# A decay column as bias of the exponential, routing tables and routed experts planned later, a scatter in two pieces

## The chip, the cores and the metric

The kernel runs on one core of a Trainium2 chip. The metric is the device time of one execution in microseconds, taken as the median of several runs.

## The reference

Two layers, each of the form x = x + attention(norm(x)) * silu(experts(norm(x))), all in float32. Layer 0 is softmax attention with eight experts. Nearly all of the change is about layer 1, on 2 x 512 tokens of width 256: linear attention by a gated delta rule, and two shared and sixteen routed experts of which each token takes two.

```python
beta  = sigmoid(x @ W_b.T)
decay = exp(-softplus(x @ W_a.T + dt_bias) * exp(A_log))     # one per token and value head
kk    = kk / norm(kk)
def step(state, inp):                    # 16 key heads, 2 value heads each, 128 x 128 states
    Sk    = k_t . state
    delta = (v_t - Sk) * b_t
    state = state * d_t + outer(k_t, delta)
    o     = q_t . state
# o is normed, multiplied by silu(z), projected by W_out
probs = softmax(xt @ W_router);  top_v, top_i = top_k(probs, 2)
routed_out = sum over the two experts of gelu(xt @ Wrt_up[e]) * gate @ Wrt_down[e]
```

## The kernel before

The scan is done in chunks of 128 tokens. A **unit** u (0 to 63) is key head h = u // 4, chunk i = u % 4, and takes both batches and both value heads at once, which makes four lanes of 128 columns. In a unit the decay between two tokens of a chunk is the exponential of a difference of running sums of logarithms: a row (the sum at one token, along the columns) plus a column (the negative sum at the other, one number for each partition). `row` fetches the rows of the four lanes from DRAM (`crow`) into RC on all partitions (L1256), `dec` adds the column `cumb` on GpSimd (L2786), puts -1e30 where the later token would come first (affine_select, L2789), and takes the exponential on ScalarE (E, L2544). `gram` multiplies keys by keys and by queries (L1612) and VectorE multiplies with E (L2232). From the result an inverse of a triangular matrix is built by doublings (L1633 to L1656, with VectorE's ZL, ZF, R, and ScalarE's XYLM), then W (L2292), and the state update (KS, U, so: L1674 to L1704, with ScalarE's D, QSc, De). Heads 0 and 1 (units 0 to 7) do all doublings unit by unit; from head 2 on the inner 16 x 16 blocks of four units are inverted together (`dg`, `iv1`, `p8`, `iv2`, `q8`, `iv3`), `xc` copies them on ScalarE (L2551), and `sx` scatters them to `parked` in DRAM by 16 DMAs of SyncE (SP; L1285), 8 blocks by 2 matrices. `ld` loads the unit's matrices back from there.

Each head needs projections of keys, queries, values and gates (L1339), three convolution taps each on VectorE (L2148), and its output projection (L1737, L1745).

The **routed experts**: `top` finds the two best experts of each token (L1807 to L1820, VectorE and one ScalarE operation), `cnt`, `own`, `tiles`, `hits`, `slot` (L1832 to L1891, VectorE, with small matmuls L1562 to L1574) make the tables that sort tokens by expert into 31 tiles. Eight groups `g` of four tiles follow: gathers of rows and weights by indirect DMAs of GpSimd (L2729, L2745), transposes (L1583), products (L1592, L1600), a gelu, and a store of the results (`ss`, L1222). At the end `cb` gathers each token's two results (L2755) and adds them up on VectorE (L2198).

**What sets the order.** All this is listed as parts with an engine, an estimated cost, what they depend on, and a rank (about the unit number beside which the part belongs). `Plan.arrange` is a list scheduler: it takes again and again the part that can begin first by its own estimates, in steps of 0.0517 us; among equals the lower rank goes first. The result is a fixed order for each engine and a fixed assignment of PSUM banks. Each engine runs its list in order and waits with semaphores. The dictionaries `RANK` and `LATER` shift the rank and the beginning of each kind of part on each engine.

```python
begin = at + self.HOLD if p.eng == "PE" and p.label[0] in self.THIN and thin > self.CAP else at
key = int((begin + p.later) * (1 / self.GRAIN)), p.rank, p.no
```

## Time and profile before

| | |
|---|---|
| runs, us | 1229.45, 1229.77, 1232.14 (median 1229.77) |
| profiled execution, us | 1230.72 |
| its span, us | 1228.9 |
| mean granted clock of TensorE | 0.982 of full |
| instructions | 28718 |
| layer 0 and the preparation of layer 1 | until about 300 us |
| units 0 to 63 | from about 300 us to the end |

The profile is of one execution; its span is the time from the first to the last recorded instruction. Engines are named PE (TensorE; PEld its weight loads), DVE (VectorE), ACT (ScalarE), POOL (GpSimd), SP (SyncE, its queue SPq). PEclk is the clock granted to TensorE as a share of full speed. "x8" is a number of instructions; in a timeline, a bracket at the end gives the engine's idle time before the instruction and what ended it. Matmuls overlap, so their single durations add up to more than their busy time.

### The profile page before, as it was taken

What the parts mean: (1) busy time and instruction counts of PE and PEld (TensorE: products, weight loads), DVE (VectorE), ACT (ScalarE), POOL (GpSimd) and SP (SyncE); (2) the same over time, 40 slices, a digit from 0 to 9 for tenths busy, and PEclk for the clock granted to TensorE, in tenths of its full rate; (3) what the DMA queues carried; (4) which work ended last, traced back from release to release, by engine and by line L of the source; (5) the groups of instructions that cost most, each with busy time, mean ns of one, the idle gap of its engine ahead of it and who ended that gap; (6) DMA issues with size and microseconds to landing.
All of it is one profiled execution on the core that took longest, in us unless ns stands there. A gap on an engine that the chain in (4) does not pass through costs nothing. (4 is left out here: it accounts for less than half of the span.)

```text
span 1228.9 us, 28718 instructions
## 1 busy us (share of the span) xinstructions
PE 1159.3 (94%) x9866; PEld 977.3 (80%) x9866; DVE 1047.5 (85%) x2365; ACT 841.6 (68%) x2396; POOL 863.4 (70%) x1101
## 2 busy tenths in 40 slices
PE   8898999888799899999999999999999999999997
PEld 7654566666698888989898988888888888888886
DVE  5796356899988989898988999899899889999988
ACT  4014643477487678877787778777877787787775
POOL 4115342839879888797969888787878787867634
PEclk9999999889799999999999999999999999999999
DMA  7942122214226556565636375655454663626331
GB/s 232 249 122 102 49 74 74 86 40 150 84 78 161 119 169 149 156 188 132 190 94 207 94 214 143 189 146 152 141 163 130 179 171 90 186 56 208 73 117 44
DMA packets 219492, 165.94 MB, mean 135 GB/s; under 512 B 103572, under 2 KB 186772, under 8 KB 219348
## 3 DMA queue, kind: packets, MB, share of 16 engines
q1 hardware_dynamic: 214612, 149.82, 44.0%
q0 software_dynamic: 4736, 14.29, 3.9%
q8 instruction: 79, 1.29, 0.4%
q14 instruction: 65, 0.53, 0.1%
HBM read 115.71 MB, written 48.16 MB: 133 GB/s over the span
## 5 line engine op out<-in xcount | busy, mean ns | idle before, releaser
L2556 ACT ACTIVATE XYLM<-ps 128x512 f16<-128x512 f32 x216 | 125.9, 598 | 54.1 <-PE ps L1647 53.1
L2148 DVE SCALAR_TENSOR_TENSOR KQ<-ps,cw,KQ 128x511 f32<-128x511 f32 (+2 forms) x192 | 140.6, 742 | 12.7 <-ACT KQ L2492 11.0
L2148 DVE SCALAR_TENSOR_TENSOR yv<-ps,cw,yv 128x511 f32<-128x511 f32 (+2 forms) x192 | 139.8, 741 | 8.6 <-ACT yv L2492 6.7
L1339 PE MATMUL ps<-XH,WVh 128*128 128x256 f32 (+1 forms) x384 | 133.5, 348 | 7.1 <-ACT KN L2507 4.5
L1339 PE MATMUL ps<-XH,WVl 128*128 128x256 f32 (+1 forms) x384 | 122.9, 320 | 0.0
L1339 PE MATMUL ps<-XL,WVh 128*128 128x256 f32 (+1 forms) x384 | 122.8, 320 | 0.0
L2590 ACT ACTIVATE sq<-O 128x128 bf16<-128x128 f32 x256 | 79.5, 310 | 28.7 <-DVE O L2328 14.5
L2596 ACT ACTIVATE O<-O,small 128x128 f32<-128x128 f32 x256 | 82.1, 400 | 14.2 <-POOL small L2834 14.0
L2278 DVE TENSOR_TENSOR ZL<-ps,cst 128x256 f16<-128x256 f32 x192 | 77.9, 415 | 10.4 <-PE ps L1633 8.9
L1339 PEld LDWEIGHTS ps<-XH,WVh 128*128 128x128 f32 x384 | 72.8, 190 | 12.8 <-ACT KN L2507 5.4
L2853 POOL TENSOR_TENSOR OGL<-O,OGH 128x512 fp32r<-128x512 f32 x62 | 80.6, 1300 | 2.8
L1704 PEld LDWEIGHTS ps<-De,PT 128*128 128x128 f32 x512 | 75.5, 193 | 5.7
L2786 POOL TENSOR_TENSOR RC<-RC,dec 128x512 f32<-128x512 f32 x64 | 67.2, 1051 | 17.0 <-DMA RC<-crow 16.8
L1704 PE MATMUL ps<-De,PT 128*128 128x128 f32 x512 | 77.8, 277 | 0.0
L1339 PEld LDWEIGHTS ps<-XH,WVl 128*128 128x128 f32 x384 | 72.5, 189 | 5.8
L1339 PEld LDWEIGHTS ps<-XL,WVh 128*128 128x128 f32 x384 | 72.9, 190 | 3.3
L2578 ACT ACTIVATE D<-ps,dec 128x128 f32<-128x128 f32 x192 | 60.9, 378 | 20.6 <-PE ps L1690 18.9
L2439 ACT ACTIVATE PT<-ps 128x1024 f32<-128x1024 f32 (+3 forms) x64 | 44.1, 705 | 43.8 <-PE ps L1436 41.8
L2834 POOL TENSOR_TENSOR small<-small 128x4 f32<-128x4 f32 (+1 forms) x66 | 67.4, 1021 | 5.5
L1737 PE MATMUL ps<-WOh,OGH 128*128 128x256 f32 x248 | 67.2, 304 | 2.9 <-DVE O L2347 2.9
L1612 PE MATMUL ps<-KQ 128*128 128x256 f32 x256 | 68.2, 389 | 0.2 <-ACT st L2604 0.2
L2565 ACT ACTIVATE QSc<-ps,dec 128x128 f32<-128x128 f32 x192 | 59.4, 377 | 13.1 <-DVE RH L2304 12.8
(359 smaller groups left out, 4083.0 us busy)
## 6 DMA issues: line engine op xcount, KB each, us to landing
XYLM<-parked SPq DMA_DIRECT2D x56, 512.0 KB, 5.3
RC<-crow SPq DMA_DIRECT2D x128, 128.0 KB, 4.7
decayed<-PTE SPq DMA_DIRECT2D x64, 256.0 KB, 3.4
PT<-decayed SPq DMA_DIRECT2D x64, 256.0 KB, 3.1
parked<-LM SPq DMA_DIRECT2D x56, 256.0 KB, 4.9
WV<-in_WV SPq DMA_DIRECT2D x16, 512.0 KB, 4.1
exr<-in_ex SPq DMA_DIRECT2D x16, 384.0 KB, 3.9
WK<-in_WK SPq DMA_DIRECT2D x16, 256.0 KB, 3.0
```

The lines of the kernel that those rows point to most:

```text
L1339: m = pe.matmul(o, a, b, start=c + k == 0, stop=c == 1 and k == 2)
L1612: m = pe.matmul(ps[:, bk, 256 * b:256 * b + 256].rearrange("p (k t) -> p k t", k=2), K[:, h % 3, at], KQ[:, h % 3, :, at], start=True, sto ...
L1704: m = pe.matmul(ps[:, bk, 256 + 128 * v:384 + 128 * v], PT[:, u % 2, 2 * b + v, :], De[:, b, v, :], start=True, stop=True)
L1737: pe.matmul(ps[:, bk, 256 * b:256 * b + 256], OGH[:, 2 * b + v, :], weights[:, h % 2, v, :], start=v + k == 0, stop=False, skip_group_chec ...
L2148: m = dve.scalar_tensor_tensor(out=dst[:, k:512], in0=ps[:, bk, 0:512 - k], scalar=cw[:, h, j, 3 - k:4 - k], in1=dst[:, k:512], op0=ALU.mu ...
L2278: leave(dve.tensor_tensor(half(zl(k), k, 0), p, lv(k), ALU.mult), "a", u, k)
L2556: leave(act.activation(changed(u, k), ps[:, bank("b", u, k), :].rearrange("p (c n t) -> p c n t", c=2, t=1 << (k - 1)), ACT.Copy), "b", u, k)
L2590: act.activation(sq[:, 1, :], O[:, u % 2, l, :], ACT.Square, accum_out=so[:, u % 2, l:l + 1]).then_inc(s_sqo, 1)
L2596: m = act.activation(O[:, u % 2, l, :], O[:, u % 2, l, :], ACT.Copy, scale=ro[:, u % 2, l:l + 1])
L2786: pool.tensor_tensor(rc.rearrange("p (b v) t -> p b v t", b=2), rc.rearrange("p (b v) t -> p b v t", b=2), bias.unsqueeze(3).broadcast_to( ...
L2834: pool.tensor_tensor(ro[:, u % 2, four], ro[:, u % 2, four], mh[:, four], ALU.pow).then_inc(s_ro, 1)
L2853: pool.tensor_tensor(OGL[:], O[:, u % 2], OGH[:].bitcast(F32), ALU.subtract).then_inc(s_ogl, 1)
```

## The change

1. `dec`: GpSimd's addition of the column is gone, and the select alone remains. ScalarE takes the exponential lane by lane, four instructions of 128x128 with the column as bias, where one of 128x512 stood; it now waits itself for the column (`s_dd`).
2. `top` moves from rank -4 to 4 and 5, the tables from rank 2 to 7, 7.5, 8, 8.5 and 8.6, the groups of routed experts from 1 + 5.5g to 9 + 5g, and the final combining from 45 to 48.
3. `sx` becomes `sx` and `sy`, each of eight DMAs (first matrix 0 of all blocks, then matrix 1), two parts in SP's list; `xc` and `ld` wait for both.
4. The estimated costs of `dec` and `sx` in the plan follow (POOL 1.83 to 0.7, ACT 0.53 to 1.08; SP 7.9 to twice 3.95), and nearly every entry of `RANK` and `LATER` has another value.

```diff
 RANK = {
-    "KS": {"ACT": 15.02}, "KS:first": {"ACT": 149.13, "DVE": 1181.68, "PE": 1010.25},
+    "KS": {"ACT": 22.36}, "KS:first": {"ACT": -215.27, "DVE": 22.74, "PE": -258.01},
...
-HEADS = ("ck", "ck1", "ck2", "ck3", "cq", "cq1", "cq2", "cq3", "cv", "cv1", "cv2", "cv3", "kn", "kb", "kns", "Vt", "Zt", "dg", "iv1", "p8", "iv2", "q8", "iv3", "xc", "sx")
+HEADS = ("ck", "ck1", "ck2", "ck3", "cq", "cq1", "cq2", "cq3", "cv", "cv1", "cv2", "cv3", "kn", "kb", "kns", "Vt", "Zt", "dg", "iv1", "p8", "iv2", "q8", "iv3", "xc", "sx", "sy")
...
-                                              rank + RANK.get(phase(label), {}).get(eng, 0.0), int(takes) if n == 0 else 0)
+                                              round(rank, 6) + RANK.get(phase(label), {}).get(eng, 0.0), int(takes) if n == 0 else 0)
...
-    P.add(("top", 1), -4, ("DVE", 1.5, (("rt1",), "DVE")), ("ACT", 1.6))
-    P.add(("top", 2), -4, ("DVE", 4.5, (("top", 1), "ACT")))
+    P.add(("top", 1), 4, ("DVE", 1.5, (("rt1",), "DVE")), ("ACT", 1.6))
+    P.add(("top", 2), 5, ("DVE", 4.5, (("top", 1), "ACT")))
...
-    P.add(("dec", u), rank, ("POOL", 1.83, (("row", u), "DMA"), (("pre", 4), "DVE")),
-          ("ACT", 0.53, earlier(1, "pt", "DVE"), (("cc", 1), "POOL")))
+    P.add(("dec", u), rank, ("POOL", 0.7, (("row", u), "DMA")),
+          ("ACT", 1.08, earlier(1, "pt", "DVE"), (("cc", 1), "POOL"), (("pre", 4), "DVE")))
...
-    P.add(("sx", h), rank + 0.2, ("SP", 7.9, (("xc", h), "ACT")), ("DMA", 0.3))
+    P.add(("sx", h), rank + 0.2, ("SP", 3.95, (("xc", h), "ACT")), ("DMA", 0.3))
+    P.add(("sy", h), rank + 0.2, ("SP", 3.95, (("xc", h), "ACT")), ("DMA", 0.3))
...
-    P.add(("own",), 2, ("DVE", 3.0, (("cnt",), "DVE")))
-    P.add(("tiles",), 2, ("DVE", 3.4, (("own",), "DVE")))
-    P.add(("hits",), 2, ("DVE", 2.4, (("tiles",), "DVE")))
+    P.add(("own",), 7.5, ("DVE", 3.0, (("cnt",), "DVE")))
+    P.add(("tiles",), 8, ("DVE", 3.4, (("own",), "DVE")))
+    P.add(("hits",), 8.5, ("DVE", 2.4, (("tiles",), "DVE")))
...
     for g in range(GROUPS):
-        rank = 1 + 5.5 * g
+        rank = 9 + 5 * g
...
-    rank = 1 + 5.5 * GROUPS
+    rank = 8 + 5 * GROUPS
...
-                        for k in range(2):
-                            sp.dma_start(parked[h % 2, k, at, :, at].rearrange("r q c -> q r c"),
-                                         XY16[at, k, :].rearrange("q (r c) -> q r c", c=16)).then_inc(d_sx, 16)
+                        sp.dma_start(parked[h % 2, 0, at, :, at].rearrange("r q c -> q r c"),
+                                     XY16[at, 0, :].rearrange("q (r c) -> q r c", c=16)).then_inc(d_sx, 16)
+                elif what == "sy":
+                    w.wait_ge(d_l1, 128)
+                    w.wait_ge(s_xc, 2 * (h - LEAD + 1))
+                    for b in range(8):
+                        at = slice(16 * b, 16 * b + 16)
+                        sp.dma_start(parked[h % 2, 1, at, :, at].rearrange("r q c -> q r c"),
+                                     XY16[at, 1, :].rearrange("q (r c) -> q r c", c=16)).then_inc(d_sx, 16)
                 elif what == "ld":
                     w.wait_ge(d_sx, 256 * ((h - OWN) // 4 + 1))
...
-                    act.activation(E[:, :, 1:129], RC[:, u % RCS], ACT.Exp).then_inc(s_E, 1)
+                    w.wait_ge(s_dd, 9)
+                    for l in range(4):
+                        c = 128 * (l // 2) + 32 * (u % 4) + 2 * (u // 4) + l % 2
+                        m = act.activation(E[:, l, 1:129], RC[:, u % RCS, l, :], ACT.Exp, bias=cumb[:, c:c + 1])
+                    m.then_inc(s_E, 1)
...
                     w.wait_ge(d_row[u % RCS], 32 * (u // RCS + 1))
-                    w.wait_ge(s_dd, 9)
-                    pool.tensor_tensor(rc.rearrange("p (b v) t -> p b v t", b=2), rc.rearrange("p (b v) t -> p b v t", b=2),
-                                       bias.unsqueeze(3).broadcast_to((128, 2, 2, 128)), ALU.add).then_inc(s_rel, 1)
-                    w.wait_ge(s_rel, nth("POOL", *x))
                     pool.affine_select(out=rc, in_=rc, compare_op=ALU.is_ge, fill=-1e30, base=0,
                                        pattern=[[0, 4], [1, 128]], channel_multiplier=-1).then_inc(s_lag, 1)
```

## Rows read from the trace of the kernel before

**Rows 1.** Page, part 1: busy time, share of the span and instructions of each engine.

```profile
PE 1159.3 (94%) x9866; PEld 977.3 (80%) x9866; DVE 1047.5 (85%) x2365; ACT 841.6 (68%) x2396; POOL 863.4 (70%) x1101
```

**Rows 2.** Windows of 50 us: length, busy time (instructions) by engine, PEclk, DMA share, GB/s.

```profile
300.00:350.00 50.00, 38.18 (x433) 33.19 (x432) 45.41 (x101) 28.08 (x82) 42.79 (x49) 0.83 0.32 89
350.00:400.00 50.00, 47.96 (x479) 42.70 (x477) 42.55 (x90) 38.29 (x108) 42.87 (x58) 1.00 0.47 124
400.00:450.00 50.00, 45.81 (x410) 41.90 (x407) 45.76 (x101) 35.55 (x109) 40.36 (x50) 0.97 0.57 149
450.00:500.00 50.00, 46.00 (x416) 40.70 (x415) 43.34 (x97) 37.13 (x109) 44.05 (x56) 1.00 0.63 172
```

**Rows 3.** Windows of other lengths, same columns.

```profile
302.70:323.30 20.60, 10.83 (x86) 9.16 (x87) 18.88 (x32) 5.32 (x18) 17.70 (x18) 0.64 0.25 77
...
323.00:350.00 27.00, 25.15 (x295) 22.19 (x293) 24.14 (x62) 20.63 (x61) 22.79 (x29) 0.96 0.36 96
600.00:1100.00 500.00, 492.04 (x4385) 437.58 (x4385) 451.87 (x1024) 389.55 (x1189) 407.19 (x517) 1.00 0.54 149
```

**Rows 4.** Timeline of VectorE: start, duration in us, operation, idle time before it.

```profile
244.66 0.28 DVE L1807 TENSOR_REDUCE small<-s 128x8 f32<-128x128 f32 x1
...
248.50 1.74 DVE L2117 RECIPROCAL dec<-dec 128x256 f32<-128x256 f32 x1
...
301.84 0.28 DVE L1832 SCALAR_TENSOR_TENSOR st<-ps,cst 128x128 f32<-128x128 f32 x1
...
309.52 0.68 DVE L2292 SCALAR_TENSOR_TENSOR W<-ps,XYLM 128x512 f32<-128x512 f32 x1
...
314.84 3.96 DVE L1891 SCALAR_TENSOR_TENSOR st<-cst,small 128x2048 f16<-128x2048 f32 x1
```

**Rows 5.** Timeline of TensorE, same columns.

```profile
251.46 0.79 PE L1339 MATMUL ps<-XH,WVh 128*128 128x512 f32 x1 [4.54 <-ACT KN L2507]
...
310.34 2.04 PE L1690 MATMUL ps<-V,W 128*128 128x128 f32 x8 [4.58 <-DVE W L2292]
...
319.20 0.40 PE L1644 MATMUL ps<-ZL,XYLM 128*128 128x64 f16 x4 [2.34 <-DVE ZL L2278]
...
364.67 1.06 PE L1690 MATMUL ps<-V,W 128*128 128x128 f32 x8
```

**Rows 6.** Tile RC (ns min/median/max, starts; waits), then ScalarE's timeline.

```profile
L2786 POOL TENSOR_TENSOR RC<-RC,dec x64: 1033/1044/1324, 265.6 to 1126.8; 128x512 f32<-128x512 f32 x64
L2789 POOL TENSOR_SCALAR_AFFINE_SELECT RC<-RC x64: 636/642/907, 266.8 to 1128.0; 128x512 f32<-128x512 f32 x64
...
  POOL RC L2789: 4.4, 6
...
281.68 0.63 ACT L2544 ACTIVATE E<-RC 128x512 f32<-128x512 f32 x1
...
324.97 1.28 ACT L2596 ACTIVATE O<-O,small 128x128 f32<-128x128 f32 x4 [0.93 <-POOL small L2834]
```

**Rows 7.** VectorE's L2148 by source line (ns min/median/max); GpSimd's timeline.

```profile
L2148 DVE SCALAR_TENSOR_TENSOR KQ<-ps,cw,KQ x192: 716/742/752, 208.5 to 1097.2; 128x511 f32<-128x511 f32 x64, 128x510 f32<-128x510 f32 x64, 128x509 f32<-128x509 f32 x64
...
316.79 2.51 POOL L2812 TENSOR_SCALAR_AFFINE_SELECT XYLM<-XYLM 128x512 f16<-128x512 f16 x1
```

**Rows 8.** Timeline of SyncE's queue: issues.

```profile
457.30 7.85 SPq L1285 DMA_DIRECT2D parked<-XY  x16
465.26 0.37 SPq L1299 DMA_DIRECT2D PT<-decayed  x1
```

**Rows 9.** Windows of L1592 alone and of L1600 alone; tile wt by line.

```profile
350.00:400.00 50.00, 2.03 (x16) 1.86 (x16) 1.00 0.47 124
...
350.00:400.00 50.00, 2.06 (x8) 1.37 (x8) 1.00 0.47 124
...
L2755 POOL DMA_INDIRECT wt<-rows_out,posi x12: 955/1033/1119, 972.6 to 1174.5; - x12
L2198 DVE SCALAR_TENSOR_TENSOR KQ<-wt,small,KQ x12: 472/482/1504, 1136.2 to 1198.2; 128x256 f32<-128x256 f32 x12
```

More of the change, by code:

```diff
@@ L134 @@
[L134 to L136 removed]
[4 rows of a table removed]
[L141 removed]
+    "KS": {"ACT": 22.36}, "KS:first": {"ACT": -215.27, "DVE": 22.74, "PE": -258.01},
+    "KS:last": {"ACT": 280.22, "DVE": 252.3, "PE": 210.41}, "U": {"ACT": 50.18},
@@ new lines @@
+    "gram:first": {"DVE": -67.68, "PE": -12.72}, "gram:last": {"DVE": -517.09, "PE": -1250.23},
+    "gt": {"ACT": 520.96, "PE": -897}, "hits": {"DVE": -53.08}, "iv1": {"DVE": -1477.56}, "iv2": {"DVE": -6.87},
+    "iv3": {"DVE": -326.24}, "kb:first": {"POOL": -503.43}, "kn": {"ACT": 206.3, "POOL": 107.57},
+    "kn:first": {"ACT": -0.06, "PE": -26.86, "POOL": 808.85}, "kns": {"ACT": 112.77},
+    "ld": {"DMA": 211.49, "SP": -612.6}, "ld:last": {"DMA": 55.72, "SP": -10.09},
+    "ln1": {"ACT": 378.5, "DVE": 269.03, "PE": -405.47}, "ls": {"DMA": -79.98},
@@ L142 @@
+    "yl:last": {"DVE": -291.41, "PE": 170.61},
 }
 LATER = {
[L146 to L150 removed]
@@ new lines @@
+    "own": {"DVE": 0.04}, "pd": {"SP": 0.18}, "pd:last": {"SP": 0.08}, "pf": {"DVE": 0.63, "SP": 2.39},
+    "pl:last": {"POOL": 0.03}, "pm:last": {"POOL": 1.31}, "ps:first": {"DMA": 1.52, "SP": 1}, "ps:last": {"SP": 0.05},
+    "py": {"POOL": 0.23}, "r:first": {"PE": 0.04}, "r:last": {"DVE": 0.13}, "rb:0": {"SP": 0.69},
+    "rc:1": {"DVE": 1.5}, "rd:0": {"SP": 0.02}, "rd:1": {"SP": 0.37}, "row:first": {"DMA": 1.39, "SP": 1.22},
+    "row:last": {"SP": 0.13}, "sc:1": {"ACT": 0.21, "PE": 0.01}, "slot": {"DVE": 0.17}, "small": {"SP": 2.48},
@@ L536, in plan_inverse @@
     if u >= OWN:
-        P.add(("ld", u), rank - 0.5, ("SP", 0.45, (("sx", h), "DMA"), earlier(3, "c", "DVE")), ("DMA", 2.2))
+        P.add(("ld", u), rank - 0.5, ("SP", 0.45, (("sx", h), "DMA"), (("sy", h), "DMA"), earlier(3, "c", "DVE")), ("DMA", 2.2))
     P.add(("pd", u), rank + 0.5, ("SP", 0.45, (("ps", u), "DMA"), earlier(2, "so", "PE", 0), earlier(2, "so", "PE", 1)), ("DMA", 0.8))
```

142 lines of the change are left out of this document (61 added, 81 removed), and 23 rows, old and new, of the table RANK.

## The prediction

> **What bounds the kernel now.** I read the page first. TensorE is busy in 94% of the span, VectorE in 85%, GpSimd in 70%, ScalarE in 68% [rows 1]. The mean hides where time is lost, so the table by stage comes next. From 600 to 1100 us TensorE is busy in 492.04 of 500 us, at a clock of 1.00 [rows 3]. There it sets the pace, VectorE being second with 90%, and GpSimd (81%) and ScalarE (78%) have room. Before that TensorE has holes: it is busy 38.18 of 50 us at 300 to 350, with a granted clock of 0.83, and misses 2.04 us of 350 to 400, 4.19 of 400 to 450 and 4.00 of 450 to 500 [rows 2]. So a change is worth something if it closes early holes, and next to nothing if it only takes load from GpSimd after 500 us.
>
> The finer windows, among which also that long one stands, put the hole at 302.7 to 323.3 us. There TensorE is busy 10.83 of 20.60 us at a mean clock of 0.64, while VectorE is busy 18.88 [rows 3]. The timeline says with what: the routing tables (L1832 to L1891) start at 301.84 and end at 318.80. Between them stand only three operations of the main work, R (0.68), W (0.68) and one ZL (0.42) [rows 4] (of the three, W is shown). TensorE's rows name them as what it waited for: W 4.58 us, ZL 2.34 us. And the matmuls that it does run go at its lower level (1.2 of 2.4 GHz): eight matmuls of L1690 take 2.04 us here and 1.06 us at 364.67 [rows 5].
>
> **The change part by part. Tables.** They are 318.80 - 301.84 = 16.96 us of VectorE less 1.78 for the three operations, 15.2 us, moved from rank 2 to ranks 7 to 8.6, that is beside units 7 to 9 instead of unit 1. The hole: 10.83 us of busy TensorE at mostly half rate is about 6.2 us at the full rate (10.83 x 1.06/2.04 = 5.6, a little more since part ran fast). In the next window, 323 to 350, TensorE is busy 25.15 of 27 us [rows 3], 93%; at that share the 6.2 us of work want 6.7, at worst twice that, because this work is a chain of dependent steps. The gain is 20.6 - 6.7 = 13.9 at best, 20.6 - 13.4 = 7.2 at worst; I take 11 us. It is passed on to the end, since TensorE afterwards is the pacemaker and what it did not do there it must do later.
>
> The same 15.2 us come back at the new place. Between 400 and 500 us VectorE has 4.24 + 6.66 = 10.9 us free and TensorE misses 8.2 us already [rows 2]. If all free time of VectorE served the tables, TensorE would pay 15.2 - 10.9 = 4.3 us; if none did, 15.2 us, if its queued matmuls of projections bridge all of it, 0. The longest piece is hits, 3.96 us, the others are parts of 2.4 to 3.4 us in the plan, so the main work gets in between them, which it got only three times before. I take 5.
>
> **Top two.** L1807 to L1820 (244.66 to 248.50, 3.84 us) stand before the reciprocal L2117 of the decay chain, which starts at 248.50, the moment they end [rows 4]. Moved to ranks 4 and 5, they let this chain start up to 3.8 us earlier. But TensorE's own stall there, 4.54 us, waits for ScalarE's KN [rows 5], and while the decays are computed it has projections to do. Gain between 0 and 3.8; I take 1, nearer to the row of KN.
>
> **Decay.** GpSimd loses L2786, 64 x 1.044 us = 67 us, and keeps the select L2789 (0.642). ScalarE has four 128x128 activations instead of one 128x512. The trace has no exponential with a bias column. The one now takes 0.63 us; nearest to the four is L2596, 128x128 with a column as scale, four in 1.28 us [rows 6]. That adds 0.65 us a unit, 64 x 0.65 = 42 us in all. The bounds: the four handle the elements of the one, so they add no less than 0, and if each took as long as the one, 1.9 us, 121 us in all; the row of L2596 has the very shape, so I take its 42. ScalarE has 110 of 500 us free [rows 3], some 215 over the 978 us after 250; 42 fit in, but the engine drains PSUM banks, and an eviction behind the four comes up to 0.65 us later. On the other side E comes 1.04 - 0.65 = 0.4 us sooner after its row has landed, the wait for the column moves from GpSimd's queue to ScalarE's (where drains of projections stand behind it, once, near 262 us), and ScalarE waited for the select only 6 times, 4.4 us in all [rows 6]. The row of unit u + 2 is fetched into the buffer that E of unit u frees, so a later E also makes that fetch later; the two offset each other within the unit. The gain is at most 4.4, the loss, if a twentieth of the added 42 us shows in TensorE's waits, 2, and if a fifth of twice that shows, 17. I take 0 net.
>
> Here a rule can be weighed. The main VectorE operation L2148 keeps within 716 and 752 ns over 192 runs, whatever GpSimd does, while GpSimd's select took 2.51 us beside hits, against 0.64 elsewhere [rows 6, 7]. So less work on GpSimd makes the taps no faster; I book 0. The Trainium skill, page "SBUF — State Buffer", section "Who interferes with whom", says that a VectorE instruction with two SBUF inputs and a GpSimd instruction that reads SBUF exclude one another for their whole length, and that one with a single SBUF input does not wait. The trace agrees with both halves. By it the tables, which read SBUF twice, would collide with GpSimd at the new place too.
>
> **Scatter in two pieces.** sx is one block of 16 issues on SP, 7.85 us at 457.30, and PT<-decayed is issued right behind it, at 465.26 [rows 8]. In two blocks (same 16 issues, same data) what is ready gets in after about 4 us, up to 3.9 us earlier. This happens 14 times, but load ld still waits for both, and may come later by whatever is put between. Bounds: the 3.9 us gained at two of the fourteen, where TensorE happens to wait for what stands behind (8), or 2 lost. I take a gain of 1.
>
> **Routed experts.** Eight groups move from ranks 1 + 5.5g to 9 + 5g, with their gathers on GpSimd's queue, four rows and four weights each, and their stores on SP's. The first group's matmuls lie between 350 and 400 us: 16 of L1592 in 2.03 us, 8 of L1600 in 2.06 [rows 9], and eight transposes, 1 us by the rate of the first. That is 5 us. Taken out of 350 to 440 us, where TensorE has holes, they go to where it is full. If nothing fills in, that costs 5 us, if projections of the next heads do, 0; I take 2. At the end, the last group moves from rank 39.5 to 44 and the combining gathers from 45 to 48, 3 units later; 64 units in the 929 us after 300 make 14.5 each, so 44 us. They begin at 972.6 now and are used from 1136.2 on [rows 9]: hidden, with 120 us of room.
>
> **Sum.** -11 + 5 - 1 + 0 - 1 + 2 = -6 us. The order of everything else is drawn anew too (nearly all of RANK and LATER); TensorE's idle time from 500 to 1200, about 10 us, bounds what that can gain, and it can lose as much; 0 to -3 is where I put it, since GpSimd, whose late work heads pieces of the chain, is freer: -2. The profiled execution took 1230.7 us (span 1228.9 and 1.8 around it; 1 more than the median of 1229.77). Against its own time the sum gives 1230.7 - 8 = 1222.7, against the median 1229.8 - 8 = 1222 us, which I forecast.
>
> **Rivals.** (A) Likeliest, the above: hole at 303 to 323 closed, part of it back at 400 to 500. (B) The stall only moves: at ranks 7 to 8.6 VectorE is 87 to 92% full, the tables cost 11 there, gain and price cancel, 1229 us. For it: VectorE's row of 400 to 450, 45.76. Against: at 302 us only the first units' chains are there to be fed, and each main result that VectorE delays stops them; at 400 us projections of later heads are queued too, and TensorE is busy 92% although VectorE is as full. (C) Slower: ScalarE becomes late. The four activations take not 1.28 but some 1.7 us, between the row and its bound, which makes 64 x 1.07 = 68 us, and they stand before drains of TensorE's banks. Once more than 8 us of it show in TensorE's waits the gain is gone; a fifth of it makes 13.6 - 8 = +5, 1235 us. For it: PSUM drains on ScalarE are what TensorE's bank waits hang on. Against: 110 of 500 us free. (D) The tables and GpSimd exclude one another at the new place, by the select's 2.51 us: three such blocks and the inner blocks of head 2 behind them delay its inverse by 3 x 1.9 = 6 us, 1228 us. The rule of the page above is this rival's. (E) Everything fits: hole closed to the best 14, the tables are free at the new place, the chain of the decays gains 3, the holes at 400 to 500 shrink by 2 more: 1211 us.
>
> **How the numbers follow.** A 0.50 (1222, its own range 1216 to 1227), E 0.17 (1211), B 0.12 (1229), C 0.15 (1235), D 0.06 (1228). The measurement tells 0.2%, 2.5 us, from no change. Faster: 0.47 of A, all of E (0.17), 0.05 of B and D, whose times have a spread too: 0.69. Same: the other 0.03 of A and 0.10 of B: 0.13. Slower: C, and 0.03 of D: 0.18. The range that leaves out 0.2 goes from 1208 to 1234.
>
> **What would show it.** TensorE busy over 45 of 50 us at 300 to 350 with a clock above 0.95; the tables' lines in pieces between 380 and 460, and TensorE missing up to 5 us more there; L2786's line gone, L2544's 64 activations become 256 of 128x128, near 0.4 us each, and ScalarE's busy time goes up by 40 to 65 us (durations overlap); the first group of experts after 430. The prediction is wrong if TensorE's total idle time does not fall, or if waits for ScalarE's drains grow by more than 10 us.

## The result: slower by 3.2%

| | before | after |
|---|---|---|
| runs, us | 1229.45 to 1237.46, median 1230.95 (4) | 1269.53 to 1272.81, median 1271.57 (4) |
| ratio to before, 95% interval | | 1.0321 [1.0292, 1.0349] |
| profiled execution and its span, us | 1230.72, 1228.9 | 1272.52, 1270.8 |
| granted clock, mean | 0.982 | 0.970 |

The forecast was 1222 us with a range to 1234. The kernel takes 1271.6, some 40 us more than before. Lines of the kernel after lie a few further on: L1704 is now L1709, L2148 is L2153, L2789 is L2792, L1891 is L1896, L2544 is L2552, L1592 is L1597.

The page, part 1 (compare [rows 1]), and the costliest group that the edit made:

```profile
PE 1171.5 (92%) x9866; PEld 985.8 (78%) x9866; DVE 1050.0 (83%) x2365; ACT 877.4 (69%) x2587; POOL 797.6 (63%) x1037
...
L2552 ACT ACTIVATE E<-RC,dec 128x128 f32<-128x128 f32 x256 | 81.9, 399 | 10.3 <-DVE PTE L2237 9.4 <-issue 0.5
```

GpSimd lost 65.8 us and ScalarE got 35.8, as the edit says. TensorE has the same 9866 matmuls, 12.2 us more busy time and 29.7 us more idle time (69.6 to 99.3).

Windows of the kernel after (compare [rows 2] and the third of [rows 3]; columns as there):

```profile
300.00:350.00 50.00, 42.96 (x485) 35.98 (x486) 47.35 (x112) 37.70 (x116) 37.95 (x52) 0.97 0.36 112
350.00:400.00 50.00, 44.57 (x487) 36.45 (x486) 43.25 (x89) 35.79 (x100) 36.97 (x49) 1.00 0.35 91
400.00:450.00 50.00, 44.97 (x357) 39.63 (x355) 38.20 (x96) 36.49 (x118) 39.20 (x46) 0.97 0.65 185
450.00:500.00 50.00, 45.85 (x420) 41.10 (x420) 39.31 (x93) 34.49 (x113) 34.58 (x45) 0.93 0.31 82
...
600.00:1100.00 500.00, 485.18 (x4284) 434.50 (x4284) 449.36 (x999) 408.21 (x1267) 381.20 (x488) 1.00 0.55 154
```

The hole at 300 to 350 did get smaller, 42.96 for 38.18, and the clock there is 0.97 for 0.83. The same holds where the tables themselves stand now (compare the first of [rows 3]):

```profile
333.10:353.70 20.60, 16.09 (x163) 13.95 (x163) 20.18 (x47) 13.28 (x44) 14.94 (x16) 0.92 0.25 72
```

Behind it things got worse, the steady stretch too: 485.18 for 492.04.

To see where the 41.9 us of span were lost, cut both traces at the same work: layer 0 until its last update of x, the preparation until the first state product of unit 0 (L1704), 286.7 us of units, the other units, the tail. Before, then after:

```profile
0.00:217.40 217.40, 201.43 (x1322) 129.76 (x1323) 142.16 (x311) 80.88 (x135) 72.93 (x93) 0.99 0.45 127
217.40:313.30 95.90, 76.06 (x517) 60.38 (x516) 84.98 (x200) 63.89 (x142) 69.37 (x101) 0.87 0.32 93
313.30:600.00 286.70, 270.05 (x2527) 241.80 (x2525) 254.30 (x572) 213.73 (x639) 242.20 (x301) 0.98 0.53 144
600.00:1217.40 617.40, 605.76 (x5476) 540.56 (x5475) 558.17 (x1267) 480.12 (x1470) 472.20 (x596) 1.00 0.51 141
```

```profile
0.00:233.70 233.70, 211.64 (x1344) 138.55 (x1344) 142.82 (x314) 83.99 (x142) 73.06 (x93) 0.93 0.43 119
233.70:326.00 92.30, 72.73 (x512) 56.65 (x513) 81.18 (x186) 63.28 (x155) 60.89 (x95) 0.91 0.30 94
326.00:612.70 286.70, 260.22 (x2399) 228.00 (x2398) 239.29 (x550) 210.12 (x656) 198.05 (x255) 0.97 0.43 123
612.70:1259.50 646.80, 620.94 (x5583) 557.60 (x5582) 579.40 (x1299) 516.82 (x1627) 459.09 (x584) 1.00 0.51 144
```

Layer 0 takes 16.3 us longer, and no line of its code was edited. The preparation gives back 3.6. The units take 933.5 us for 904.1, 29.4 more: in their first 286.7 us TensorE is idle 26.5 for 16.65 and gets 128 matmuls less done, in the others 25.9 for 11.6. So two thirds of the loss lie in the loop, spread over it, and a third in layer 0 and the preparation, whose code the change doesn't touch; it draws their order anew too.

In layer 0 the clock is 0.93 for 0.99, and 10.2 of the 16.3 us are longer busy time, a part of it because 22 more matmuls fall into the window (1344 for 1322). Windows of 10 us of the kernel after show the places; before, the same windows have 0.83, 1.00 and 1.00:

```profile
50.00:60.00 10.00, 6.16 (x33) 4.09 (x28) 4.61 (x8) 0.60 (x1) 5.58 (x6) 0.64 1.06 237
...
120.00:130.00 10.00, 7.08 (x60) 3.14 (x58) 2.93 (x6) 3.11 (x7) 4.58 (x6) 0.73 0.11 33
130.00:140.00 10.00, 9.33 (x56) 4.08 (x52) 3.48 (x5) 8.27 (x13) 3.54 (x5) 0.59 0.15 42
```

The waits say what the loop lost (engine, line, releaser: us in total, times, longest). Before:

```profile
POOL RC L2786 <- DMA RC<-crow: 16.8, 13, 3.7
...
POOL OGH L2847 <- DVE O L2347: 6.2, 4, 3.6
...
POOL LM L2806 <- DMA parked<-LM: 3.3, 2, 1.9
```

After:

```profile
POOL OGH L2850 <- DVE O L2352: 69.5, 26, 9.8
POOL RC L2792 <- DMA RC<-crow: 51.1, 21, 5.6
...
POOL LM L2809 <- DMA parked<-LM: 17.0, 7, 6.1
...
PE ps L1742 <- POOL OGH L2850: 10.8, 6, 5.4
```

GpSimd stands 26 times, up to 9.8 us, before the cast of O into OGH, because its list has the cast before O is there; what is queued behind it comes late. (Before, it stood at this cast 28.5 us in all, 22.3 of them until L1745 had let go of OGH.) TensorE's output projection L1742 waits for OGH 10.8 us in turn (before, its L1737 never did). Added up by what ended them, TensorE's waits for GpSimd grow from 4.9 to 22.9 us, those for VectorE from 36.5 to 40.2, for ScalarE from 20.8 to 24.0 and for DMAs from 1.3 to 3.1: GpSimd's share is 18.0 of the 29.7 us of added idle time. Once, at 1109 us, LM waits for a store, the second half of O stands behind it, and TensorE behind that (GpSimd's timeline, then TensorE's):

```profile
1109.34 0.61 POOL L2809 CAST LM<-M 128x512 f16<-128x512 f32 x1 [6.07 <-DMA parked<-LM]
1109.91 1.26 POOL L2856 TENSOR_TENSOR OGL<-O,OGH 128x512 fp32r<-128x512 f32 x1
...
1111.23 1.22 PE L1750 MATMUL ps<-WOh,OGL 128*128 128x256 f32 x4 [3.80 <-POOL OGL L2856]
```

And the tables? VectorE's timeline (compare [rows 4]):

```profile
263.58 1.74 DVE L2122 RECIPROCAL dec<-dec 128x256 f32<-128x256 f32 x1
...
333.10 0.28 DVE L1837 SCALAR_TENSOR_TENSOR st<-ps,cst 128x128 f32<-128x128 f32 x1
...
348.77 0.68 DVE L2352 TENSOR_TENSOR O<-ps,Z 128x512 f32<-128x512 f32 x1
349.37 0.68 DVE L2368 TENSOR_TENSOR xt<-ps,xt 128x512 f32<-128x512 f32 x1
349.96 2.31 DVE L1896 SCALAR_TENSOR_TENSOR st<-cst,small 128x2048 f16<-128x2048 f32 x1
```

They stand at 333 to 352 us, not between 380 and 460, so beside units 0 and 1, not 7 to 9. Of the shift by 31 to 35 us against [rows 4], 12.7 are the later start of the units. Top two still stands right before the reciprocal of the decay chain, which starts 15.1 us later than before.

### The profile page after: what moved, and what is told of

Same layout as the page of the kernel before. It is cut to its first block, busy times and chain, and to the rows that moved or that the text cites. A ratio compares the mean times of both kernels' runs of the same rounds, so it can differ in the third digit from the quotient of the medians.

```text
span 1270.8 us, 28912 instructions
## 1 busy us (share of the span) xinstructions
PE 1171.5 (92%) x9866; PEld 985.8 (78%) x9866; DVE 1050.0 (83%) x2365; ACT 877.4 (69%) x2587; POOL 797.6 (63%) x1037
## 4 chain that ended last, share of the span: by engine, by line
PE 42%; DVE 21%; DMA 10%; ACT 9%; POOL 7%; issue 7%; SPq 4%; DVEq 0%; POOLq 0%; ACTq 0%
PE ps L1344 14%; DMA parked<-LM 4%; DVE yv L2153 4%; PE ps L1742 2%; PE ps L1695 2%; DMA RC<-crow 2%; PE ps L1709 2%; DVE KQ L2153 2%; ACT E L2552 2%; DVE Mp L2032 2%; PE ps L1452 2%; DVE M L2237 1%; PE ps L1652 1%; PE ps L1649 1%; DVE PTE L2237 1%
## 5 line engine op out<-in xcount | busy, mean ns | idle before, releaser
L2153 DVE SCALAR_TENSOR_TENSOR KQ<-ps,cw,KQ 128x511 f32<-128x511 f32 (+2 forms) x192 | 140.8, 743 | 13.0 <-ACT KQ L2497 10.5
L2153 DVE SCALAR_TENSOR_TENSOR yv<-ps,cw,yv 128x511 f32<-128x511 f32 (+2 forms) x192 | 140.6, 742 | 6.9 <-ACT yv L2497 4.7
L2552 ACT ACTIVATE E<-RC,dec 128x128 f32<-128x128 f32 x256 | 81.9, 399 | 10.3 <-DVE PTE L2237 9.4
L2850 POOL CAST OGH<-O 128x512 fp32r<-128x512 f32 x62 | 38.2, 616 | 71.2 <-DVE O L2352 69.5
L1709 PE MATMUL ps<-De,PT 128*128 128x128 f32 x512 | 79.3, 278 | 0.0
L1709 PEld LDWEIGHTS ps<-De,PT 128*128 128x128 f32 x512 | 74.6, 191 | 5.2 <-ACT De L2590 0.2
L1742 PE MATMUL ps<-WOh,OGH 128*128 128x256 f32 x248 | 67.8, 305 | 11.3 <-POOL OGH L2850 10.8
L2792 POOL TENSOR_SCALAR_AFFINE_SELECT RC<-RC 128x512 f32<-128x512 f32 x64 | 41.1, 642 | 51.6 <-DMA RC<-crow 51.1
```

The lines of the kernel that those rows point to most:

```text
L1709: m = pe.matmul(ps[:, bk, 256 + 128 * v:384 + 128 * v], PT[:, u % 2, 2 * b + v, :], De[:, b, v, :], start=True, stop=True)
L1742: pe.matmul(ps[:, bk, 256 * b:256 * b + 256], OGH[:, 2 * b + v, :], weights[:, h % 2, v, :], start=v + k == 0, stop=False, skip_group_chec ...
L2153: m = dve.scalar_tensor_tensor(out=dst[:, k:512], in0=ps[:, bk, 0:512 - k], scalar=cw[:, h, j, 3 - k:4 - k], in1=dst[:, k:512], op0=ALU.mu ...
L2552: m = act.activation(E[:, l, 1:129], RC[:, u % RCS, l, :], ACT.Exp, bias=cumb[:, c:c + 1])
```

## Experiments

Each kernel's ratio is to runs of the kernel before on the same chip. "Layer 0" is the end of its last update of x and "loop" the time from the first to the last state product, both in the kernel's one profiled execution; "O" and "RC" are GpSimd's waits for O (before the cast to OGH) and for the rows in RC, in us. "Numbers" are the dictionaries RANK and LATER.

| kernel | median us | ratio, interval | layer 0 | loop | O | RC |
|---|---|---|---|---|---|---|
| before | 1230.95 | 1 | 217.4 | 904.1 | 6.2 | 16.8 |
| after | 1271.57 | 1.0321 [1.0292, 1.0349] | 233.7 | 933.5 | 69.5 | 51.1 |
| decay_same_order | 1235.39 | 1.0035 [1.0006, 1.0063] | 216.3 | 907.1 | 7.2 | 31.0 |
| old_with_new_tables | 1354.37 | 1.1014 [1.0980, 1.1049] | 231.8 | 1009.1 | 48.9 | 31.3 |
| new_with_old_tables | 1260.58 | 1.0239 [1.0205, 1.0273] | 219.9 | 928.0 | 26.7 | 52.8 |
| ranks_only | 1240.99 | 1.0093 [1.0059, 1.0127] | 216.2 | 912.3 | 17.9 | 25.0 |
| decay_replanned | 1264.30 | 1.0261 [1.0217, 1.0306] | 221.7 | 932.3 | 12.2 | 58.8 |
| scatter_split_only | 1251.74 | 1.0175 [1.0146, 1.0204] | 221.9 | 923.2 | 14.0 | 14.0 |
| tables_really_late | 1265.85 | 1.0292 [1.0264, 1.0320] | 221.1 | 942.9 | 4.8 | 34.0 |
| new_maxima_first | 1275.60 | 1.0354 [1.0308, 1.0400] | 235.0 | 943.2 | 72.2 | 59.2 |
| main_work_first | 1231.48 | 1.0001 [0.9976, 1.0025] | 220.5 | 906.9 | 6.2 | 16.5 |
| new_order_old_decay | 1285.75 | 1.0444 [1.0407, 1.0481] | 232.3 | 950.4 | 64.4 | 39.2 |
| new_later_taken_back | 1278.49 | 1.0395 [1.0350, 1.0440] | 233.1 | 933.2 | 61.9 | 51.0 |
| decay_retuned | 1241.63 | 1.0091 [1.0064, 1.0118] | 228.2 | 912.2 | 8.6 | 48.2 |
| edits_in_old_lists | 1240.51 | 1.0060 [1.0038, 1.0081] | 223.9 | 909.0 | 8.0 | 32.5 |
| layer0_taken_back | 1315.47 | 1.0659 [1.0628, 1.0690] | 221.7 | 989.6 | 44.9 | 60.8 |
| changed_retuned_a | 1245.81 | 1.0110 [1.0087, 1.0134] | 228.1 | 905.0 | 16.2 | 47.8 |
| changed_retuned_b | 1243.26 | 1.0106 [1.0076, 1.0137] | 215.4 | 907.1 | 7.5 | 45.6 |
| new_numbers_retuned | 1264.68 | 1.0266 [1.0237, 1.0295] | 224.8 | 938.7 | 68.5 | 60.0 |

### The decay edit in the old lists

`decay_same_order` has the new instructions of `dec` and the costs of before, so that all lists are those of before.

```diff
-act.activation(E[:, :, 1:129], RC[:, u % RCS], ACT.Exp).then_inc(s_E, 1)
+for l in range(4): m = act.activation(E[:, l, 1:129], RC[:, u % RCS, l, :], ACT.Exp, bias=cumb[:, c:c + 1])
-pool.tensor_tensor(... rc ..., bias.unsqueeze(3).broadcast_to((128, 2, 2, 128)), ALU.add)
```

> The kernel before with the decay edit alone (no addition on GpSimd, four activations with the column as bias on ScalarE), and the plan's costs left as they were, so that every engine runs its list of before in the same order. Theory O (the loss is in the redrawn order of the lists, not in what the edits do): the time stays within 6 us of before, 1225 to 1236. Theory S (ScalarE's added 36 us of work costs TensorE's waits, the rival C of the prediction): 1240 to 1265, with TensorE waiting for ScalarE by at least 10 us more after 600 us.

It loses 0.35%, about 4 us. ScalarE has 878.0 us, GpSimd 797.2, as in the kernel after, so the cost of the moved work is this 4, not 40. A part of it is seen in the waits of its profile:

```profile
POOL small L2830 <- ACT sq L2594: 58.1, 36, 6.2
...
POOL RC L2787 <- DMA RC<-crow: 31.0, 23, 3.8
```

ScalarE's squares (sq), which stand behind the four activations, come later, and GpSimd, with less to do, stands 58.1 us for 28.8 before; TensorE's waits for ScalarE's O are 9.3 us for 6.1. All of TensorE's waits for ScalarE add up to 27.1 us for 20.8. That is rival C's mechanism at about a third of its price (4 us of 13.6).

### Numbers and edits taken apart

`old_with_new_tables` is the kernel before with the numbers of after, `new_with_old_tables` the kernel after with those of before.

```diff
 RANK = {
-    "KS": {"ACT": 15.02}, "KS:first": {"ACT": 149.13, "DVE": 1181.68, "PE": 1010.25},
+    "KS": {"ACT": 22.36}, "KS:first": {"ACT": -215.27, "DVE": 22.74, "PE": -258.01},
...
```

> The kernel before, with RANK and LATER of the changed kernel and nothing else. Theory O: clearly slower than before, 1255 or more, with the 16 us of layer 0 (last product of layer 0's attention at about 217 us, not 201) all there, since nothing but these numbers acts there. Theory S: near before, below 1240.

> The changed kernel, with RANK and LATER of the kernel before. Theory O: layer 0 is as fast as before (attention's last product near 201 us), which gives back 16 us; the loop may still be slower than before, since the changed costs of dec and sx make another order of it: 1235 to 1260. Theory S: at least 1255, the loss of the loop being that of the changed kernel.

With the numbers of the other kernel the unedited one takes 1354 us. With the old numbers the changed one takes 1261, 11 us less than with its own. The second lies where its two expectations overlap and decides nothing between them. So neither part is good with the other's partner: numbers and costs belong together. And the numbers, not the edits, bring two features of the kernel after: layer 0's end at 232 to 235 us (224.8 only in `new_numbers_retuned`), and GpSimd's long waits for O (48.9 to 72.2 us in the six kernels with the new RANK, at most 26.7 with the old one; `layer0_taken_back`, which mixes them, has 44.9).

### The base ranks alone

`ranks_only` is the kernel before with the new base ranks of top, tables, groups and combining.

```diff
-    P.add(("hits",), 2, ("DVE", 2.4, (("tiles",), "DVE")))
+    P.add(("hits",), 8.5, ("DVE", 2.4, (("tiles",), "DVE")))
...
-        rank = 1 + 5.5 * g
+        rank = 9 + 5 * g
```

> The kernel before with the base ranks of top, tables, experts and combining moved as in the change, RANK, LATER and all code of the engines as before. The prediction's step said that the tables go to units 7 to 9 and the hole at 303 to 323 us closes: then hits (L1891) starts after 380 us and the time falls to 1215 to 1228. The rival reading of the scheduler: the rank decides only among parts that can begin in the same step of 0.0517 us, and the entries of RANK are larger by a hundredfold, so the tables stay where they are (hits near 315 us), the hole stays, and only the experts' groups go later: 1228 to 1240.

VectorE's timeline:

```profile
314.47 3.95 DVE L1891 SCALAR_TENSOR_TENSOR st<-cst,small 128x2048 f16<-128x2048 f32 x1
```

Against 314.84 in [rows 4], a rank higher by 6.5 moves hits by nothing. The first products of experts stay too (358.7 us for 359.4); only the last ones go, from 958.2 to 1024.7. It costs 0.9%: these parts break ties elsewhere, and the lists behind change.

### One replanned edit at a time

`decay_replanned` adds the new costs of `dec` to `decay_same_order`; `scatter_split_only` is the kernel before with the third edit and its costs.

```diff
-    P.add(("dec", u), rank, ("POOL", 1.83, (("row", u), "DMA"), (("pre", 4), "DVE")), ...
+    P.add(("dec", u), rank, ("POOL", 0.7, (("row", u), "DMA")), ...
```

```diff
-    P.add(("sx", h), rank + 0.2, ("SP", 7.9, (("xc", h), "ACT")), ("DMA", 0.3))
+    P.add(("sx", h), rank + 0.2, ("SP", 3.95, (("xc", h), "ACT")), ("DMA", 0.3))
+    P.add(("sy", h), rank + 0.2, ("SP", 3.95, (("xc", h), "ACT")), ("DMA", 0.3))
```

> The kernel before with the decay edit and, beside it, the two changed costs of dec in the plan (and the column as a dependency of ScalarE's part). The engines execute exactly the instructions of decay_same_order; only the order of the lists is drawn anew by the changed costs. Theory O (the loss is in redrawn orders): slower than decay_same_order by 10 to 30 us, 1245 to 1265. Theory R (the plan helps once its costs are right): at or below decay_same_order's 1235.

> The kernel before with sx in two parts alone (plan and code), other numbers as before. Instructions and data are the same, the order of all lists is redrawn from head 2 on, since two parts of 3.95 stand for one of 7.9. Theory O: slower by 5 to 25 us, 1237 to 1257, up to about 440 us of the execution as before. The prediction's step: 1231, a gain of 1.

The same instructions cost 0.35% in the old lists and 2.6% once the plan may redraw them with truer costs. The scatter alone gives 1.75%. Each small change of a cost sends the scheduler down another path, and the path of before was better than every one of them.

### Is a later place of the tables good at all?

`tables_really_late` makes the tables wait, in the plan, for the last product of unit 3.

```diff
-    P.add(("cnt",), 2, ("PE", 0.75, (("top", 2), "DVE"), (("cc", 1), "POOL")), ...
+    P.add(("cnt",), 2, ("PE", 0.75, (("top", 2), "DVE"), (("cc", 1), "POOL"), (("so", 3, 1), "PE")), ...
```

> The kernel before, where the first part of the routing tables (cnt) depends on the state update of unit 3, so that they can't start before it; nothing else changed. This does what the ranks were meant to do. The prediction's step: the hole at 303 to 323 us closes, units 0 to 3 come 7 to 14 us sooner, and 0 to 15 us are paid at the new place. Theory O adds that the redrawn order costs 5 to 20 us later in the loop. Together 1225 to 1245; by the prediction's sum alone 1223.

Its windows (compare [rows 2]):

```profile
300.00:350.00 50.00, 48.04 (x526) 42.34 (x525) 42.19 (x102) 35.81 (x104) 44.84 (x60) 0.97 0.34 81
350.00:400.00 50.00, 46.35 (x467) 39.27 (x465) 48.27 (x107) 37.48 (x114) 40.57 (x55) 0.97 0.45 122
400.00:450.00 50.00, 40.45 (x320) 35.38 (x320) 45.30 (x82) 27.18 (x80) 35.24 (x40) 0.93 0.47 124
450.00:500.00 50.00, 38.73 (x301) 33.36 (x302) 34.45 (x86) 26.99 (x89) 36.61 (x45) 0.83 0.46 130
```

The first window is full as the prediction had it, 48.04 us at 0.97, and unit 3 has its O (L2347) at 371.82 us for 399.02, 27.2 us earlier than before. All of it is gone at unit 8, which is 8.9 us late, and the kernel takes 1265.9 us, 21 more than the top of its expectation. The hole has moved to 400 to 500 us, where TensorE is busy 79.2 of 100 us, for 91.8 before. Its waits there, in total, times, longest:

```profile
PE ps L1644 <- DVE ZL L2278: 8.2, 5, 4.3
PE ps L1633 <- DMA XYLM<-parked: 3.0, 1, 3.0
PE ps L1664 <- DVE R L2284: 2.6, 1, 2.6
```

Most of the gain is gone before any unit needs a block of head 2. By the same O, unit 4 is 30.2 us ahead, unit 5 15.3, unit 6 8.8 and unit 7 2.9. Beside these units stand the tables now, with hits from 415.00 to 418.67 us:

```profile
410.00:420.00 10.00, 5.07 (x25) 3.37 (x24) 9.90 (x10) 3.46 (x9) 8.66 (x7) 1.00 0.15 48
```

In these 10 us TensorE does 25 matmuls, for 81 in the same window before, and waits for VectorE's R. Counted from 300 us, it is 81 matmuls ahead of the kernel before at 400 us and 9 behind at 450. That is the mechanism of the prediction's rival B, the stall that only moves. Then comes a gate: units from 8 on need head 2's inner blocks, which come back from DRAM first at 432.4 us, for 430.9 before, so an earlier unit 3 does not fetch them earlier. How much of the gain each of the two takes, and how much the redrawn order behind them, no run here tells. The experts' first products come at 524.4 us for 359.4.

### Main work ahead of the tables, in otherwise old lists

`main_work_first` puts nine neighbouring parts of VectorE's list in another order.

```diff
-own, c 0, tiles, a 1 6, hits, a 1 7, so 0 0, so 0 1, slot
+c 0, a 1 6, own, so 0 0, so 0 1, a 1 7, tiles, hits, slot
```

> The kernel before with every list as it is but VectorE's, in which nine neighbouring parts change places: W of unit 0 (c 0), two ZL of unit 1 and both state updates of unit 0 go ahead of the tables' parts between which they stood. The hole at 303 to 323 us shrinks: W no longer waits for the parts own, the state update not for tiles and hits. The prediction's step (what is saved in the hole is passed on to the end one to one): units 0 to 3 come 4 to 8 us sooner and the end 4 to 8 us sooner, 1221 to 1225. The rival (a gate: units 8 and up can't start before the inner blocks of head 2 are loaded back, first at 430.9 us, whatever units 0 to 7 have gained): the first units come 4 to 8 us sooner, but that first load (L1292 in the kernel before) stays near 430 and at most 1 to 2 us reach the end, 1227 to 1229.

TensorE's timeline (compare [rows 5]):

```profile
311.38 2.05 PE L1695 MATMUL ps<-V,W 128*128 128x128 f32 x8 [0.88 <-DVE W L2297]
...
325.11 0.61 PE L1579 MATMUL ps<-st 128*128 128x32 f16 x16 [6.66 <-DVE st L1896]
```

The wait for W fell from 4.58 to 0.88 us. TensorE's own list has the matmuls of slot where they were, and there it now waits 6.66 us for hits. The window of 300 to 350 is no fuller (35.78 us), the time is the same. Unit 0 has its O at 333.18 us for 328.57, 3.1 of it from a later end of layer 0: the first units came no sooner, so this run tests neither the passing on nor the gate. Moving parts in one engine's list alone moved the stall to TensorE, which still had the matmuls of slot in their old place.

### Layer 0, and the two kinds of numbers

`new_maxima_first` is the kernel after with one fetch of weights put behind the store of the maxima on SP. In after, that store is issued at 85.19 us behind two fetches of 13.77 us, for 81.38 before. `new_later_taken_back` is after with the old LATER, `new_order_old_decay` is after in its own lists with GpSimd's addition and the single activation of before.

```diff
+_sp = ORDER1["SP"]; _sp.remove(("fx", 7)); _sp.insert(_sp.index(("max", 0)) + 1, ("fx", 7))
```

```diff
-LATER                                          # of after
+LATER                                          # of before
```

```diff
-for l in range(4): m = act.activation(E[:, l, 1:129], RC[:, u % RCS, l, :], ACT.Exp, bias=cumb[:, c:c + 1])
+act.activation(E[:, :, 1:129], RC[:, u % RCS], ACT.Exp).then_inc(s_E, 1)
+pool.tensor_tensor(... rc ..., bias.unsqueeze(3).broadcast_to((128, 2, 2, 128)), ALU.add)
```

> The changed kernel, where in SyncE's list alone the fetch of expert tile 7 (fx 7), which stands ahead of the row maxima of batch 0 (max 0) and waits for the down products of the experts, goes behind them, as in the kernel before. If this one place of the queue starts layer 0's attention late, the maxima are stored some 3 us sooner (at 82, not 85.19) and the end comes 2 to 6 us sooner, 1266 to 1270. If the attention's loss of 16 us is spread over many places, less than 1 us is to be seen at the end.

> The changed kernel with its own RANK but LATER of the kernel before, to split the 16 us of layer 0. If LATER makes them, attention's last product comes near 201 us (217.2 in the changed kernel); if RANK, near 215. The end follows the redrawn loop: 1245 to 1275.

> The changed kernel with all its lists, but the decay done as before: the addition on GpSimd, one activation of 128x512 on ScalarE. It takes the decay edit out of the changed kernel at an unchanged order. If ScalarE's four activations were the loss, 1240 or less. Theory O: the edit itself costs or gives a few us only, 1265 to 1280 (the addition is back in GpSimd's queue, whose list was made for its absence).

The place of the fetch is not the cause: the maxima are stored at 83.75 us, 1.4 sooner, and the kernel takes 1275.6 us, layer 0 no shorter. Nor is LATER: 1278.5 us, layer 0 at 233.1. And in the new lists the bias edit is worth 14 us (1285.8 without it, 1271.6 with it), where it costs 4 in the old ones. An edit has no price of its own here; it has one in each list.

`layer0_taken_back` puts the old numbers of layer 0's parts into the kernel after.

```diff
-RANK, LATER                                    # those of after
+RANK, LATER                                    # of before for tp, fx, p1, sc, mk, pv, oc, rd, ...; else those of after
```

> The changed kernel with those entries of RANK and LATER that belong to layer 0's attention and experts as they were in the kernel before. Layer 0's last PV product should come near 201 us again instead of 217.2. Theory (what is lost early is passed on to the end): 1271.6 - 16 = 1256 us, between 1250 and 1262. Rival (a gate in between swallows it: the units wait for tables, blocks loaded back, or rows of a list that is drawn anew behind): less than 5 of the 16 us reach the end, 1267 to 1277 us.

Both theories fall. Layer 0 is back at 221.7 us, 12 less, and the loop takes 989.6 us, 56 more. The scheduler places the units' parts after what layer 0's lists leave free, so probably the later numbers no longer fit the earlier lists; this is not shown. The tables come latest of all here, hits at 425.60 us, and late too in `old_with_new_tables`, the slowest kernel, at 401.17. Whether the late tables make most of the loss of these two is not tested.

### Tuning the numbers again

`decay_retuned` is `decay_replanned`, `changed_retuned_a` and `_b` are `new_with_old_tables` (all edits of the change, old numbers), and `new_numbers_retuned` is the kernel after, each with RANK and LATER changed by many small random steps (their number stands in the expectations), kept where the order did not get longer by the plan's own estimates.

```diff
-RANK, LATER                                    # as the kernel that it starts from
+RANK, LATER                                    # after many small random steps; nothing else differs
```

> The same as decay_replanned (decay edit and its costs in the plan), with RANK and LATER changed by some hundred small random steps of which those were kept that made the plan's own end earlier; no instruction is added or removed, only the lists' order. Theory O: most of the loss of decay_replanned (35 us) is gone, 1230 to 1245. If the loss were in the decay edit or its costs, 1255 to 1265 as there.

> The whole change (bias, scatter in two pieces, new base ranks, new costs), started from the RANK and LATER of before (which gave 1260.6 us) and changed in some 7,700 small random steps, each kept when the plan's own end did not get later. Theory (the drawn order costs, not the edits): within 1% of before, 1225 to 1245 us. Rival (the edits cost in any order, above all the later tables and experts and the longer ScalarE part): 1255 us or more, because the order is as good by its plan as that of before and only the edits are left.

> The same start, other random steps, an order that the plan holds for nearly as good as changed_retuned_a's. Theory as there: 1225 to 1250 us, within 10 us of changed_retuned_a. Rival (what the plan does not see, such as waits for rows of RC, transfers and the clock, decides): the two lie more than 15 us apart.

> The changed kernel with its own RANK and LATER as the start and some 7,900 small steps by the same rule, of which few were kept: its numbers were near the best of their neighbourhood by the plan already. Theory (the new numbers lie in a bad neighbourhood that the plan itself holds for about as good): 1260 to 1275 us, little changed from 1271.6. Rival (the numbers of the change are only badly tuned): below 1250 us.

The decay kernel came down from 1264.3 to 1241.6 us. The whole change came down from 1260.6 to 1245.8 and 1243.3, 26 and 28 us under the kernel after with the same edits, the same base ranks and the same costs: the rival of `changed_retuned_a`, 1255 us or more, is out (its 1245.8 is 0.8 above the top of the theory's range, too). TensorE's waits for GpSimd, 22.9 us in the kernel after, are 12.4 and 2.1 in the two. From the new numbers as the start it reached 1264.7 only. The two tunings have loops of 905.0 and 907.1 us, as good as before's 904.1 within what one profile tells, and hits at 320.80 and 312.20 us: these two orders put the tables about where the kernel before has them. Waits of the kernel `changed_retuned_b`:

```profile
POOL RC L3078 <- DMA RC<-crow: 45.6, 25, 4.7
...
POOL OGH L3136 <- DVE O L2638: 7.5, 5, 4.5
```

The long waits for O are gone, those for RC stay: they are the bias edit's (31.0 even in the old lists), where GpSimd, rid of the addition, gets to the select before the rows have landed. With 45.6 us of them the loop is as short as before's, so they cost TensorE little.

### All edits of instructions in the old lists

`edits_in_old_lists` is `decay_same_order` with the scatter in two pieces, the second one place later in SP's list where what stood behind the scatter is a fetch.

```diff
+_at = _sp.index(("sx", _h)) + 1
+if _sp[_at][0] in ("pd", "fWV", "fWK", "fWO"): _at += 1
+_sp.insert(_at, ("sy", _h))
```

> The kernel before with both edits of instructions, the exponential with the column as bias and the scatter in two pieces, in the lists of before: the second piece stands right behind the first, or one place later where what follows is a fetch of PT or of a weight (11 of 14 heads). Theory (the redrawn order is what costs): ratio 1.000 to 1.006, 1230 to 1238 us, since the decay edit alone gave 1.0035 in these lists and the scatter moves one issue by 3.9 us. Rival (the split scatter costs by itself, as the 1.0175 of its replanned kernel would say if it were not the order): above 1.012, over 1245 us.

1.0060 [1.0038, 1.0081]: about 7 us for everything that the change does to instructions; by the ratio the top of the theory's range, far from the rival's 1.012. The scatter's share would be 0.25%, but this interval and that of `decay_same_order` overlap.

## Why the prediction was wrong

Of the 3.2%, 39.5 us, the experiments put 0.6%, about 7 us, on the edited instructions (`edits_in_old_lists`), some 0.5%, 6 us, on what the whole change keeps with tuned numbers (1.0110 and 1.0106), and the other 2.1%, 26 us, on the numbers that the change came with: the two tuned kernels and the kernel after differ in nothing but RANK and LATER. TensorE's total idle time rose by 29.7 us, where the prediction wanted it to fall; its waits for ScalarE rose by 3.2, less than the 10 that it named as a sign of being wrong.

- **"The order of everything else is drawn anew too ... -2".** This is the step that failed, by its size and its sign. I bounded it by TensorE's idle time from 500 to 1200 us, about 10 us (12.1 by the trace), and said that it can lose as much. Idle time bounds a gain; it doesn't bound a loss. Redrawn lists alone gave +11 (`ranks_only`), +22 (`scatter_split_only`, its instructions included), +28 (`decay_replanned` less `decay_same_order`, 0.0226 of 1230) and +125 (`old_with_new_tables`). None gave a gain over the kernel before. In the change itself the term measured +26 us against the tuned numbers and +32 against the old lists (1.0321 less 1.0060), not -2. It was the largest term of the change, and "nearly every entry of `RANK` and `LATER` has another value" stood in the description of the change.
- **"Moved from rank 2 to ranks 7 to 8.6, that is beside units 7 to 9".** Wrong. The key of the scheduler is the beginning in steps of 0.0517 us, then the rank with RANK's entry added, and those entries run to hundreds and thousands (KS:first has 1181.68). A base rank is a tie-break among such numbers. The tables came 31 to 35 us later and `ranks_only` moved hits by 0.4 us. So -11 and +5 were sums for a move that did not take place, and the same holds for the top two and the first group of experts (400.1 us; I had it after 430).
- **"It is passed on to the end".** Wrong as well, where the move was made. `tables_really_late` gained 27.2 us at unit 3 and had lost them by unit 8, the greater part beside the tables' new place (units 5 to 7), the rest where units wait for blocks that do not come sooner. TensorE's idle time at 400 to 500 us grew by 12.6 us (20.8 for 8.2), where the prediction had put 5; a redrawn order is mixed in. That TensorE is the pacemaker from 500 us on does not say that all before it is a queue of work that only waits for TensorE.
- **The hole itself** was read rightly: 48.04 of 50 us busy at clock 0.97 once the tables are out. But hits was taken for 3.96 us of work; 1.68 of them are a wait for GpSimd (see below).
- **Decay.** The size was right: E takes 81.9 us for 40.5, 41.4 more for my 42, ScalarE in all 35.8. The net 0 was 4 in the old lists (1.0035). Rival C has the mechanism, but was not the reason: TensorE's waits for ScalarE's O went from 6.1 to 9.0 us in the kernel after.
- **Scatter, experts, combining.** The scatter's 1 is inside what could be measured in the old lists. The combining gathers came at 1059.7 us for 972.6 and stayed hidden, used from 1174.2 on.
- **Port (rival D).** The mechanism is there at the new place, once: see below. Its 6 us are not to be seen in TensorE's waits.

The Trainium skill's page "SBUF — State Buffer", section "Who interferes with whom", which the prediction weighed, is borne out here once more (below); nothing in the runs makes it a part of the 40 us.

Two things stay open. One is why layer 0 is slower with the new RANK: it ends at 231.8 to 235.0 us in five of six profiles, where the old layer-0 lists end between 216.3 and 223.9. In the kernel after, part of it goes with the clock: against `edits_in_old_lists`, which had 0.94 there, it is 9.8 us and not 16.3. One place on SP and LATER are excluded. The other is how much of the 0.5% of the tuned kernels over `edits_in_old_lists` is due to the new ranks, and how much to tuning that is not finished.

## What to carry to other kernels

Where a scheduler draws the order from estimated costs, a change of one cost or rank can change every list; before costing the edit, build it in the old order and in the new one, and count the second as a change of its own. The order of this kernel before is a point that redraws after one small change missed by 0.9 to 2.6%, so the loss to expect from a redraw was far larger than the idle time that a gain could come from. And before closing a hole, ask what the work that made it will hold up at its new place, and whether the next gate behind, here blocks loaded back from DRAM at 430 us, moves along.
